# Local attention in two six-layer stacks: the score banks' band mask written by ScalarE, and another order of a step's work

## The reference, cut to what matters

```python
def local_attention(q, k, v):            # per head
    bq = q.reshape(b, h, nw, 32, d)      # windows of 32
    bk2, bv2 = look(bk), look(bv)        # window before + own: 64 keys
    mask = (it < jb) | (it > jb + 32) | (jb == -1)
    sim = jnp.einsum('bhwie,bhwje->bhwij', bq, bk2) * 8.0
    sim = jnp.where(mask, -max, sim)
    attn = jax.nn.softmax(sim, -1)
    out = jnp.einsum('bhwij,bhwje->bhwie', attn, bv2)
for i in range(6):
    x = attn_layer(shift_tokens(x), ...) + x   # l2-normed, rotated q and k
    x = ffn_layer(shift_tokens(x), ...) + x    # layer norm, gated gelu, 341 wide
```

## Time and profile before

| what | us |
|---|---|
| median of three runs | 5445.46 |
| the profiled execution, own time | 5438.05 |
| its span | 5436.3 |
| PE busy in the span | 4737.4 (87%) |
| PE's weight loads busy | 3032.6 (56%) |
| DVE busy | 4133.6 (76%) |
| ACT busy | 3352.3 (62%) |
| POOL busy | 2735.3 (50%) |

### The profile page before, as it was taken

One profiled execution on the slowest core, in us unless ns is written; L12 is line 12 of the kernel. 1 busy time (PEld: TensorE's weight loads), 2 busy tenths in 40 slices (PEclk: granted clock), 3 DMA queues, 4 the chain that ended last, 5 costly groups with the idle time before them and its releaser, 6 DMA issues. The chain is left out here.

```text
span 5436.3 us, 135547 instructions
## 1 busy us (share of the span) xinstructions
PE 4737.4 (87%) x51446; PEld 3032.6 (56%) x51638; DVE 4133.6 (76%) x8982; ACT 3352.3 (62%) x7201; POOL 2735.3 (50%) x3646
## 2 busy tenths in 40 slices
PE   4775899999999999777777778658999999999997
PEld 2232566666666666434444344335666666666665
DVE  5897677777777777479898999966777777777774
ACT  2432677777777777444545444435777777777775
POOL 1221666666666666223233333316666666666663
PEclk7898999999999999988888889869999999999999
DMA  0000222222222222100000000002222223222221
GB/s 18 0 0 12 75 71 71 68 69 69 78 62 74 67 76 63 27 15 2 2 2 2 1 2 2 2 1 79 67 73 65 77 62 79 65 74 67 76 63 40
DMA packets 162491, 247.18 MB, mean 45 GB/s; under 512 B 36228, under 2 KB 56640, under 8 KB 161734
## 3 DMA queue, kind: packets, MB, share of 16 engines
q1 hardware_dynamic: 161862, 238.65, 16.9%
HBM read 36.15 MB, written 1.05 MB: 7 GB/s over the span
## 5 line engine op out<-in xcount | busy, mean ns | idle before, releaser
L940 POOL TENSOR_TENSOR f_rope<-f_rope,f_t 128x1024 f32<-128x1024 f32 x384 | 905.7, 2359 | 524.2 <-DVE f_t L854 524.2
L953 POOL TENSOR_TENSOR f_rope<-f_rope,f_rn 128x1024 f32<-128x1024 f32 x384 | 730.6, 1903 | 56.7 <-POOL f_rn L932 2.6
L490 PE MATMUL psum<-f_wqkv,f_xs 128*128 128x512 f32 x1536 | 729.6, 598 | 22.6 <-DVE f_t L854 22.6
L859 DVE TENSOR_REDUCE f_ss<-f_sq 128x16 f32<-128x1024 f32 x384 | 459.9, 1198 | 335.9 <-ACT f_sq L721 333.0
L1827 POOL TENSOR_SCALAR tk_scores<-tk_scores,tk_m 128x408 f32<-128x408 f32 (+28 forms) x232 | 239.2, 1031 | 783.2 <-DVE tk_m L1787 619.3
L684 ACT ACTIVATE f_kT<-psum 64x512 f32<-64x512 f32 (+1 forms) x960 | 485.3, 525 | 83.4 <-PE psum L481 73.8
L721 ACT ACTIVATE f_sq<-psum 128x1024 f32<-128x1024 f32 x384 | 393.3, 1024 | 218.7 <-PE psum L490 218.3
L854 DVE TENSOR_TENSOR f_t<-psum,f_rot 128x1024 f32<-128x1024 f32 x384 | 466.0, 1213 | 0.0
L850 DVE TENSOR_TENSOR f_rope<-psum,f_rot 128x1024 f32<-128x1024 f32 x384 | 465.3, 1212 | 0.0
L876 DVE TENSOR_REDUCE f_den<-f_prob 128x16 f32<-128x1024 f32 x192 | 234.2, 1220 | 296.0 <-ACT f_prob L726 296.0
L490 PEld LDWEIGHTS psum<-f_wqkv,f_xs 128*128 128x128 f32 x1536 | 279.3, 192 | 305.9 <-issue 298.7
(11 more groups left out here) (240 smaller groups left out, 9759.7 us busy)
## 6 DMA issues: line engine op xcount, KB each, us to landing
f_v<-f_v_tok SPq DMA_DIRECT2D x1152, 128.0 KB, 2.4
f_v<-f_v_tok SPq DMA_DIRECT2D x768, 64.0 KB, 2.0
f_wqkv<-in_Wqkv SPq DMA_DIRECT2D x36, 512.0 KB, 4.0
f_wo<-in_Wo SPq DMA_DIRECT2D x12, 512.0 KB, 4.0
f_w<-in_W SPq DMA_DIRECT2D x12, 341.0 KB, 3.3
f_w<-in_W SPq DMA_DIRECT2D x24, 64.0 KB
tk_wkv<-in_Wkv SPq DMA_DIRECT2D x1, 1024.0 KB
out<-y_tok SPq DMA_DIRECT2D x4, 256.0 KB, 2.5
```

The source lines that it names most:

```text
L490: last = pe.matmul(psum[:, n, :], xs[:, j % 2, :], wqkv[:, INNER * which + 512 * n:INNER * which + 512 * (n + 1)], start=True, stop=True)
L859: dve.tensor_reduce(ss[:, H * half:H * (half + 1)], sq[:, half, :, :], AX_X, ALU.add).then_inc(s[f"{name}_ss"], 1)
L940: pool.tensor_tensor(part, part, t2[:, half, :, :], ALU.add).then_inc(s[f"{name}_added"], 1)
L953: pool.tensor_tensor(part, part, rn[:, H * half:H * (half + 1)].unsqueeze(2).to_broadcast([P, H, DH]), ALU.mult).then_inc(s[f"{name}_norme ...
```

## The change

Three things are changed in `ffn_stack`, and nothing outside of it. ACT writes the band mask into both score banks with one copy (`seeded`), in place of PE's two products, in every step but the first scored one of a stack; the products of `weigh` start a new accumulation only in the first of four neighbouring blocks of a bank. PE's step is put in another order: turned keys come ahead of turned probabilities, and, but for j=2, the output product ahead of the weighing. ACT's step follows it: the copies into kT come ahead of those into probT; at j=2 the second and third gelu come one behind the other, ahead of the copies of the queries.

```diff
 turn_prob:                      # waits of bank n
-    if on(g, 3): wait(pe, f"ot{n}_evac", ...)  else: wait(pe, f"qt{n}_evac", ...)
+    if on(g, 1): wait(pe, f"kt{n}_evac", ...)  else: wait(pe, f"ot{n}_evac", ...)
 turn_keys:
-    if on(g, 2): wait(pe, f"pt{n}_evac", ...)
+    if on(g, 3): wait(pe, f"ot{n}_evac", ...)  else: wait(pe, f"qt{n}_evac", ...)
 turn_queries:
-    wait(pe, f"kt{n}_evac", ...)
+    if on(g, 2): wait(pe, f"pt{n}_evac", ...)  else: wait(pe, f"kt{n}_evac", ...)
 weigh:
-    probT..., v2..., start=True, stop=True)
+    probT..., v2..., start=(c % 4 == 0), stop=True, skip_group_check=True)
 score:
-    wait(pe, "on_done", through(g, 2))
-    for half in range(2):
+    wait(pe, "seeded", g - 1)
+    for half in range(0 if on(g, 2) else 2):
         pe.matmul(psum[:, 4 + half, :], k.ident_bf, k.band...)
 order of PE's step:
-    values keys turn_prob  feed|gated(0) turn_keys weigh [gated(1)] turn_queries queries
-        j==2: gated(2) score output      else: output score
+    values keys turn_keys  feed|gated(0) turn_prob
+        j==2: gated(1) weigh gated(2) turn_queries queries output score
+        else: output weigh turn_queries queries score
     turn_output
 order of ACT's step:
-    ... exponent, square k, [evacuate(1) at j==2], probT x2, [evacuate(0) at j!=2], [gelu 0], kT, [gelu 1], ...
+    ... exponent, square k, [evacuate(1) at j==2], kT, [evacuate(0) at j!=2], [gelu 0], probT x2, [gelu 1, gelu 2, table], ...
     qT x2
+    wait(act, "on_done", through(g, 2))
+    copy(sc_bank, band of the tile, one row block repeated for all heads).then_inc(s["seeded"], 1)
     ... square q
```

More of the change, by code:

```diff
@@ L335, in ffn_stack @@
                   "qt0_full", "qt1_full", "qt0_evac", "qt1_evac", "ot0_full", "ot1_full", "ot0_evac", "ot1_evac",
-                  "scores", "top", "sub_done", "exp_done", "summed", "rden_done", "pv_done", "on_done", "wo_full", "wo_evac", "res_done",
+                  "seeded", "scores", "top", "sub_done", "exp_done", "summed", "rden_done", "pv_done", "on_done", "wo_full", "wo_evac", "res_done",
                   "ff_in", "ff_mean", "ff_centred", "ff_squared", "ff_var", "ff_x", "ff_logged", "ff_y", "ff_polish", "ff_rstd", "ff_wide", "ff_scaled",
@@ L574, in turn_prob @@
                             for n in range(2):
-                                if on(g, 3):
+                                if on(g, 1):
+                                    wait(pe, f"kt{n}_evac", through(g, 1))
+                                else:
                                     wait(pe, f"ot{n}_evac", through(g, 3))
-                                else:
-                                    wait(pe, f"qt{n}_evac", through(g, 2))
                                 turn(T0 + n, prob, 8 * n, f"pt{n}_full")
@@ L584, in turn_keys @@
                             for n in range(2):
-                                if on(g, 2):
-                                    wait(pe, f"pt{n}_evac", through(g, 2))
+                                if on(g, 3):
+                                    wait(pe, f"ot{n}_evac", through(g, 3))
+                                else:
+                                    wait(pe, f"qt{n}_evac", through(g, 2))
                                 turn(T0 + n, rope[:, (j - 1) % 2, 1, :, :], 8 * n, f"kt{n}_full")
@@ L592, in turn_queries @@
                             for n in range(2):
-                                wait(pe, f"kt{n}_evac", through(g, 1))
+                                if on(g, 2):
+                                    wait(pe, f"pt{n}_evac", through(g, 2))
+                                else:
+                                    wait(pe, f"kt{n}_evac", through(g, 1))
                                 turn(T0 + n, rope[:, (j - 1) % 2, 0, :, :], 8 * n, f"qt{n}_full")
@@ L604, in weigh @@
                                     last = pe.matmul(psum[WIN * w:WIN * (w + 1), 4 + c // 4, (c % 4) * P:(c % 4 + 1) * P],
-                                                     probT[:, c, WIN * w:WIN * (w + 1)], v2[:, j % 2, w, :, c, :], start=True, stop=True)
+                                                     probT[:, c, WIN * w:WIN * (w + 1)], v2[:, j % 2, w, :, c, :],
+                                                     start=(c % 4 == 0), stop=True, skip_group_check=True)
                             last.then_inc(s["pv_done"], 1)
@@ L626, in score @@
                                 wait(pe, f"qt{n}_evac", through(g, 1))
+                            sj = (j - 1) % 4
                             if on(g, 2):
-                                wait(pe, "on_done", through(g, 2))
-                            sj = (j - 1) % 4
-                            for half in range(2):
+                                wait(pe, "seeded", g - 1)
+                            for half in range(0 if on(g, 2) else 2):
                                 pe.matmul(psum[:, 4 + half, :], k.ident_bf[:, :], k.band[:, int(sj == 0), :, :].rearrange("p h w -> p (h w)"),
@@ L652, in step @@
                     keys()
-                    turn_prob()
+                    turn_keys()
                     if f is not None and j == 2:
@@ L657, in step @@
                         feed({0: "mean", 1: "wide", 3: "out"}.get(j))
-                    turn_keys()
-                    weigh()
+                    turn_prob()
                     if f is not None and j == 2:
                         gated(1)
-                    turn_queries()
-                    queries()
-                    if f is not None and j == 2:
+                        weigh()
                         gated(2)
+                        turn_queries()
+                        queries()
+                        output()
                         score()
-                        output()
                     else:
                         output()
+                        weigh()
+                        turn_queries()
+                        queries()
                         score()
@@ L743, in step @@
                         evacuate(1)
[L744 to L752, removed]
                     if on(g, 1):
@@ L766, in step @@
                             last.then_inc(s[f"kt{n}_evac"], 1)
+                    if j != 2:
+                        evacuate(0)
+                    if f is not None and j == 2:
+                        gelu(0)
+                    if on(g, 2):
+                        wait(act, "pv_done", through(g, 3))
+                        for n in range(2):
+                            wait(act, f"pt{n}_full", through(g, 2))
+                            copy(flat4(probT, n), psum[:, T0 + n, :]).then_inc(s[f"pt{n}_evac"], 1)
                     if f is not None and j == 2:
                         gelu(1)
+                    if f is not None and j == 2:
+                        gelu(2)
+                        act.preload_act_table_set(EXP_LN)
                     if j != 2 and on(g, 0):
@@ L774, in step @@
                             copy(flat4(qT, n), psum[:, T0 + n, :]).then_inc(s[f"qt{n}_evac"], 1)
+                    if on(g, 1) and on(g, 2):
+                        wait(act, "on_done", through(g, 2))
+                        mask = k.band[:, int((j - 1) % 4 == 0), 0:1, :].to_broadcast([P, H, 2 * WIN])
+                        copy(sc_bank, mask).then_inc(s["seeded"], 1)
                     if f is not None and j == 0:
@@ L784, in step @@
                         act.activation(xn[:, :], xn[:, :], ACT.Identity, bias=layer_vec(k.ln_b, ff[0]), scale=layer_vec(k.ln_g, ff[0])).then_inc(s["ff_gained"], 1)
-                    if f is not None and j == 2:
-                        gelu(2)
-                        act.preload_act_table_set(EXP_LN)
                     if j == 2 and on(g, 0):
```

## The result

The changed kernel takes 6026.94 us (median of 4 runs, 6024.93 to 6035.36) against 5442.56 us (4 runs, 5436.67 to 5449.53): a ratio of 1.107, 95% interval 1.1057 to 1.1083. The profiled execution took 6035.36 us, its span is 6033.5.

What follows compares the result with a forecast made beforehand. PE bounds the kernel before; a longer loop through ACT and DVE takes over. 5438 us plus 460 for two stacks gives 5898; with 130 for falls of PE's clock, the stated forecast is 6025, range 5850 to 6185.

Steps and rivals of the forecast that it cites:

- the loop that takes over: From one weighing to the next through PE, ACT and DVE: 14.7 us before, 18.6 after, against PE's own 15.65.
- One sign that was named: PE would stand idle ahead of the output product, released by a copy of values.
- The term of 0.59: ACT's second copy of values, behind the copies into kT, lies on the loop ahead of the output product: 0.59 us.
- The plain loop, 18.6: Step ending with j=0: 4.79 + 6.96 + 0.96 + 0.91 + 2.42 + 0.59 + 1.95 = 18.6 us between weighings.
- j=1, j=2, j=3: Steps ending with these weighings take 19.1, 20.95 and 21.3 us; with j=0, 79.95 against 70.33 a sequence.
- The loop without falls, 5898: Rival: the longer loop holds in both stacks, adding 460 us, and PE's clock never falls: 5898 us, chance 25%.
- The clock, 130 us: PE's clock falls after the gap around turned probabilities in half of 190 steps, 1.37 us each: 130 us, ends 0 and 260.
- two unlike rows: Earlier PE stretches: 1.34 us of work in 3.10, then clock 0.51; 0.95 in 3.40, clock stayed 1.00.
- The rival of a fall in every step (6158): The longer loop holds and PE's clock falls in every step: 6158 us, chance 20%.
- The mask's copy, 1.05 us and nothing in a plain step: ACT's copy runs from 3.77 to 4.8 us after the weighing, when the square of queries was due anyway; ends nothing and 2.1.
- Transfers, none: Landing of the spread values ahead of ACT's first copy of values: 0 to 0.2 us a step, at most 30; none taken.
- a gain only while PE sets the step: Mask products leaving PE save 0.36 us in 190 steps, 68 us; rival with PE still the bound: 5370, chance 5%.

Runs made afterwards that it cites:

- the kernel whose clock held: Changed kernel with idle bf16 products ahead of the turned probabilities, only at j=0, j=2 and in steps without a feed-forward part: 5906.18 us, ratio 1.0846.
- the mask alone: Kernel before, in its old order, with ACT's mask copy in place of PE's two mask products: 5459.31 us, ratio 1.0018.
- both moves: Mask copy in the old order, DVE's division moved earlier at j=2, ACT's square of queries ahead of the variance's at j=0: 5391.96 us, ratio 0.9906.

## Why the prediction was right, point by point

- **What bounds the kernel, and the loop that takes over:** right. PE's idle time lies where it was said, ahead of the turned probabilities, released by ACT's copies into kT (113.4 of the 202 us that the view of PE's waits adds up to; 55 more lie ahead of the gate's products at j=2). The two orders undone one at a time show that each of them moves the loop over PE's work. One sign that was named did not show: PE has no idle time ahead of the output product, since the second half of the turned probabilities fills it. The term of 0.59 for the copy of values fits as a length, but no run shows that this copy, rather than those probabilities, holds the output product.
- **The plain loop, 18.6:** 18.68 at j=0 in the kernel whose clock held; in the changed kernel every step that ends with j=0 had a fall and took 19.6 to 20.7. Its terms, predicted and measured at j=1 (there with ACT's square for the variance in the first): 4.79 and 5.01, 6.96 and 6.97, 0.96 and 0.96, 0.91 and 0.90, 2.42 and 2.43, 0.59 and 0.65, 1.95 and 1.98. All could be taken from the trace before, though no step there was limited by this loop. That the output product replaces the copies into probT, and isn't added to them, shows in the timeline (1542.17 against 1543.23) and in the sum, which would be 19.7 with both.
- **j=1, j=2, j=3:** 19.1, 20.95 and 21.3 predicted; 18.90, 21.12 and 21.50 measured. The first overlap was larger than taken, the longer chains a little slower; sum 80.2 against 79.95.
- **The loop without falls, 5898:** 5906, by the kernel whose clock held.
- **The clock, 130 us:** 121, and that it came so close is in part luck. Half of the steps was the middle of two unlike rows; 77 of 190 had a fall, and which ones goes by the kind of step (all at j=0, half at j=2), which the forecast did not foresee. A fall cost 121 / 77 = 1.57 us in the mean rather than 1.37: fewer falls, each dearer. In the steps shown it was 1.49 at j=0 (20.17 less 18.68), lost in the output product and not in turned probabilities and weighing as forecast, and 1.80 at j=2 (22.92 less 21.12). With 130 the forecast's own terms add up to 6028, not 6025, and its upper end to 6188, not 6185, which changes nothing. The rival of a fall in every step (6158) would be the rule of the Trainium skill ("TensorE: Matmul & The Clock Gate", section "Why this matters for your kernels") taken for each gap. The trace agrees with its direction: idle products in the gap hold 1.00. It doesn't agree that each gap costs: 23 of the 44 steps that end with j=2 stayed at 1.00, as did the step that ends at 1543.23, with the feed-forward product in the gap.
- **The mask's copy, 1.05 us and nothing in a plain step:** 1.036 us, and the scores waited for it twice in 1900 us. With the order as changed it costs 31 us in all (18.68 to 18.90 at j=1, 21.06 to 21.51 at j=3).
- **Transfers, none:** right. ACT's first copy of values waited 1.47 us for its landing in the step shown, and the exponential behind it still waited 0.52 us for DVE, so the transfer set nothing there. In the first stack the exponential starts 11.75 or 11.76 us after the weighing in 42 of the 45 steps that end with j=0 or j=2, the forecast's 11.75.
- **Where the reasoning fell short** of the forecast's own question: "a gain only while PE sets the step", 68 us. With the order before, where PE does set the step, the mask alone gained nothing. The wait for the division is a wait that the copy brings to ACT, and the prediction named only the square of the queries and the scores behind it, by the plain step's division at 3.77 us. At j=2 the division itself is queued behind a product that waits for ACT's gelu. The experiment's expectation, 5365, has the same error, and it left out the square for the variance at j=0; with both moves 53 of the 68 us came.

## What to carry to other kernels

When an order is turned around to feed a full engine, add up the loop that runs back to it through the in-order engines, start to start, from stretches of the old trace in which nothing else is late; here PE had 16 us of work, that loop 14.7, and two moves of 2 to 3 us were each enough to replace the bound, while busy shares showed room on every engine. When a piece of work is handed to another engine, look at what that engine's new wait is queued behind on the third engine, in each kind of step and not in the plain one alone. And an engine that waits for short bursts can be worth filling with idle work, but only in steps in which it has time to spare.

## What the runs showed of the hardware

- A copy by ACT from SBUF to PSUM, 128 x 1024, whose source is one bf16 block of 64 columns repeated 16 times, took 1027 to 1037 ns, against 1002 to 1028 for ACT's squares of 1024 columns that lie in line. No plain copy of that width from SBUF to PSUM stands beside it. The group of the mask's copies (by tile, ACT, changed kernel: lowest, median and highest ns, first and last start, form):

```profile
L692 ACT ACTIVATE psum<-band x190: 1027/1036/1037, 580.8 to 5965.0; 128x1024 f32<-128x1024 bf16 x190
```

- PE's products add to numbers that ACT has written to PSUM, here a mask that isn't zero, 190 times. The weighing before them in the same bank starts a new accumulation only in the first of four neighbouring blocks in each bank. The Trainium skill ("PSUM — Partial Sum Buffer", section "The four PSUM rules") says that such a product adds to what ACT wrote where an earlier product has marked the element as written, and overwrites it where a new start has left it unmarked, so that zero alone is safe either way. The runs agree as far as the adding goes; the marks are in no trace, and the copy without the altered start of the weighing was not tried.
- Steps with the same list of products on PE were granted 1.00 throughout or fell: of the 44 that end with j=2, 23 and 21. In the step j=0 shown above the 3.5 us from the turned probabilities on were granted 0.51. Idle bf16 products ahead of both halves of them, in the steps j=0 and j=2, kept a whole stretch of 1800 us at 1.00, worth 121 us of 6027.
